# Dense layer 2: a third buffer of rounded and low parts, and rounding shared among three engines

## The reference

```python
edge_feat = gelu((x[src] + edge_attr) @ W_pre + b_pre) * bases
y = x + segment_sum(edge_feat, dst)
h = relu(bn(y @ W1 + b1))
h = relu(bn(h @ W2 + b2))          # bn: mean and variance over all nodes
x = layernorm(x + (y + h))
# second layer: messages over the edges by relation, a gate, an MLP, layernorm
```

## Time and profile before

| what | value |
| --- | --- |
| median of 3 runs | 2010.78 us (2007.58 to 2014.62) |
| the profiled execution's own time | 2016.65 us |
| its span, first to last instruction | 2014.9 us |
| mean granted TensorE clock | 0.962 of full speed |
| dense layer 2 in the span | about 626 to 934 us |
| GpSimd's last scatter | 678.64 us |

### The profile page before, as it was taken

How to read it: one execution, slowest core, us unless ns; L and a number is a source line. 1 busy time by engine, 2 the same in 40 slices (tenths; PEclk the granted TensorE clock), 3 DMA queues, 4 the chain that set the end, 5 groups by cost and what they waited for, 6 DMA issues and landing times. The chain is left out here.

```text
span 2014.9 us, 27432 instructions
## 1 busy us (share of the span) xinstructions
PE 1791.8 (89%) x8697; PEld 1398.7 (69%) x8697; DVE 1601.0 (79%) x2326; ACT 1295.1 (64%) x1818; POOL 1075.1 (53%) x1200
## 2 busy tenths in 40 slices
PE   4677589999998999999999999956999999999994
PEld 3465478888886776766666666635888888888883
DVE  4688456766767999997999999994888888888883
ACT  1434246566656898886888888862566666666663
POOL 7556446776785400001555555557776566654443
PEclk8899789999999999999999999987999999999997
DMA  9999999999995899994999999965654423222210
GB/s 343 368 352 393 363 357 339 337 342 330 342 236 135 244 350 343 333 344 157 351 388 384 389 412 392 385 247 137 174 157 138 118 89 92 92 83 79 65 41 29
DMA packets 190577, 516.22 MB, mean 256 GB/s; under 512 B 26757, under 2 KB 80111, under 8 KB 190178
## 3 DMA queue, kind: packets, MB, share of 16 engines
q1 hardware_dynamic: 132898, 389.66, 52.7%
q0 software_dynamic: 47136, 73.62, 16.2%
q10 hardware_dynamic: 10400, 51.20, 6.6%
HBM read 328.87 MB, written 241.07 MB: 283 GB/s over the span
## 5 line engine op out<-in xcount | busy, mean ns | idle before, releaser
L618 POOL DMA_INDIRECT scratch_y<-sums,k_target x196 | 313.4, 1599 | 156.1 <-issue 70.2
L1040 ACT ACTIVATE d_o<-d_u,d_free 128x256 f32<-128x256 f32 x392 | 203.1, 589 | 64.6 <-POOL d_free L1077 64.4
L1014 PEld LDWEIGHTS d_pN<-k_ident,d_r 128*128 128x128 f32 x1568 | 192.1, 193 | 52.1 <-issue 46.4
L1009 PE MATMUL d_pN<-d_y,d_free 128*128 128x512 f32 x392 | 192.0, 612 | 33.3 <-DVE d_u L1103 29.3
L821 ACT ACTIVATE d_part_h<-pT 128x1024 fp32r<-128x1024 f32 x98 | 100.5, 1026 | 150.7 <-PE pT L788 137.0
L1014 PE MATMUL d_pN<-k_ident,d_r 128*128 128x128 f32 x1568 | 192.7, 277 | 4.9 <-ACT d_r L1029 4.9
L882 DVE TENSOR_TENSOR d_part_l<-pT,d_part_h 128x1024 fp32r<-128x1024 f32 x98 | 119.9, 1225 | 85.8 <-ACT d_part_h L821 85.8
L1074 POOL TENSOR_TENSOR d_free<-d_free,k_minus_half 128x8 f32<-128x8 f32 (+1 forms) x100 | 163.6, 1636 | 0.2
L1103 DVE SCALAR_TENSOR_TENSOR d_u<-d_pN,d_free,k_base 128x256 f32<-128x256 f32 x392 | 161.0, 474 | 0.0
L256 POOL DMA_INDIRECT k_ring<-in_x,k_src x100 | 123.6, 1236 | 66.5 <-PE pT L284 37.8
L60 PE MATMUL pU<-d_part_h,k_w_h 128*128 128x512 f32 x296 | 125.9, 425 | 26.7 <-DVE d_part_l L882 13.7
(11 more groups left out here) (232 smaller groups left out, 5192.6 us busy)
## 6 DMA issues: line engine op xcount, KB each, us to landing
scratch_h<-d_h SPq DMA_DIRECT2D x168, 512.0 KB, 5.7
out<-d_o SPq DMA_DIRECT2D x97, 520.0 KB, 5.9
k_ring<-scratch_y SPq DMA_DIRECT2D x98, 512.0 KB, 7.8
d_y<-scratch_y SPq DMA_DIRECT2D x98, 512.0 KB, 7.7
scratch_y<-in_x ACTq DMA_DIRECT2D x25, 2000.0 KB, 20.2
d_h<-scratch_h SPq DMA_DIRECT2D x90, 512.0 KB, 7.0
k_ring<-scratch_h SPq DMA_DIRECT2D x78, 512.0 KB, 5.3
attr<-in_attr_t SPq DMA_DIRECT2D x25, 512.0 KB, 15.2
```

What stands on the lines that cost most here:

```text
L618: pool.indirect_dma_start(out=A["y"], out_offset=bass.IndirectOffsetOnAxis(ap=K.target[:, t:t + 1], axis=0), in_=K.sums[:, t], in_offset=N ...
L1009: pe.matmul(pN[k % 4][:, 2 * two:2 * two + 2].rearrange("p j f -> p (j f)"), twice[:], y[:, k % 4, two * 2 * F:(two + 1) * 2 * F], start=T ...
L1014: last = pe.matmul(pN[k % 4][:, j, cc * P:(cc + 1) * P], r[:, k % 4, cc, j * P:(j + 1) * P], K.ident[:], start=False, stop=j % 2 == 1 and ...
L1040: last = act.activation(o[:, k % 4, j, 0:F], u[:, k % 3, j], ACT.Identity, bias=nb[:, n, j:j + 1], scale=rs[:, n, J + j:J + j + 1])
```

## The change

From the first block of layer 2 on, there are three buffers of rounded and low parts instead of two, picked by (g - 98) % 3. The third pair, `third_h` and `third_l`, lies in the place of `sums`, behind the 64 tiles that hold blocks (tiles 64 to 71). Block 100, the first to use it, waits until the second scatter of these tiles has landed. A rounding waits for the product of three blocks before (`product` at g - 2) in place of that of two.

From the sixteenth block on (g >= 114), blocks with g % 3 == 1 are rounded by GpSimd instead of VectorE: 27 blocks, from 115 to 193. These copies stand in GpSimd's queue behind the last scatter and ahead of its last waits for them. VectorE's `parts` waits for GpSimd's semaphore there, as it does for ScalarE's, and does the low part of all blocks as before.

```diff
+POOL_FROM = 16
...
     part_h, part_l, h, held, r, _ = K.shared_second
+    third_h, third_l = K.shared_parts
...
-    hi2_scalar, hi2_vector = sem("hi2_scalar"), sem("hi2_vector")
+    hi2_scalar, hi2_vector, hi2_pool = sem("hi2_scalar"), sem("hi2_vector"), sem("hi2_pool")
...
+    def hi_on_pool(g):
+        return g % 3 == 1 and g >= NB + POOL_FROM
...
+    def parts_of(g):
+
+        at = (g - NB) % 3 if layer2(g) else g % 2
+        return (part_h[:, at], part_l[:, at]) if at < 2 else (third_h[:], third_l[:])
+
+    def wait_part(engine, g):
+
+        if g >= NB + 3:
+            engine.wait_ge(product, g - 2)
+        elif g == NB + 2:
+            for q in range(4):
+                engine.wait_ge(halved_in[q], 16 * (HELD_SUMS + 2))
+        else:
+            engine.wait_ge(product, g - 1)
...
         for t in range(early, ET):
             take_back(t)
+        for g in range(NB, 2 * NB):
+            if hi_on_pool(g):
+                pool.wait_ge(relu_done, g - NB + 1)
+                wait_part(pool, g)
+                pool.tensor_copy(parts_of(g)[0], r[:, g % 2]).then_inc(hi2_pool, 1)
...
         def hi2(g):
             if hi_on_scalar(g):
                 act.wait_ge(relu_done, g - NB + 1)
-                act.wait_ge(product, g - 1)
-                act.activation(part_h[:, g % 2], r[:, g % 2], ACT.Copy).then_inc(hi2_scalar, 1)
+                wait_part(act, g)
+                act.activation(parts_of(g)[0], r[:, g % 2], ACT.Copy).then_inc(hi2_scalar, 1)
...
         def parts(g):
             on_scalar = sum(hi_on_scalar(n) for n in range(NB, g + 1))
+            on_pool = sum(hi_on_pool(n) for n in range(NB, g + 1))
             if hi_on_scalar(g):
                 dve.wait_ge(hi2_scalar, on_scalar)
+            elif hi_on_pool(g):
+                dve.wait_ge(hi2_pool, on_pool)
             else:
                 dve.wait_ge(relu_done, g - NB + 1)
-                dve.wait_ge(product, g - 1)
-                dve.tensor_copy(part_h[:, g % 2], r[:, g % 2]).then_inc(hi2_vector, 1)
-                dve.wait_ge(hi2_vector, g + 1 - NB - on_scalar)
...
+                wait_part(dve, g)
+                dve.tensor_copy(parts_of(g)[0], r[:, g % 2]).then_inc(hi2_vector, 1)
+                dve.wait_ge(hi2_vector, g + 1 - NB - on_scalar - on_pool)
+            high, low = parts_of(g)
+            dve.tensor_tensor(out=low, in0=r[:, g % 2], in1=high.bitcast(F32), op=ALU.subtract).then_inc(lo_done, 1)
...
-            (K.sums,), K.shared_sums = same_place(
+            (K.sums,), (_, *K.shared_parts), K.shared_sums = same_place(
                 nc.sbuf_tensor, (("sums", [P, S.TC, F], F32),),
+                (("d_ahead", [P, HELD_SUMS * J * F], F32), ("d_third_h", [P, C, B], F32R), ("d_third_l", [P, C, B], F32R)),
```

More of the change, by code:

```diff
@@ L661, in dense12 @@
     early = ET * 3 // 4
-    assert HELD_SUMS * J <= early
+    assert (HELD_SUMS + 2) * J <= early
     passes = [(1, k) for k in range(NB)] + [(2, (NB - HOLD + n) % NB) for n in range(NB)]
@@ L803, in multiply @@
                     last = mm3(pe, bank(g)[:, oc], (K.w0_h[:, w, ic, cols], K.w0_l[:, w, ic, cols]),
-                               (part_h[:, g % 2, ic], part_l[:, g % 2, ic]), ic == 0, ic == C - 1)
+                               (high[:, ic], low[:, ic]), ic == 0, ic == C - 1)
             last.then_inc(product, 1)
@@ L886, in parts @@
             on_scalar = sum(hi_on_scalar(n) for n in range(NB, g + 1))
+            on_pool = sum(hi_on_pool(n) for n in range(NB, g + 1))
             if hi_on_scalar(g):
                 dve.wait_ge(hi2_scalar, on_scalar)
+            elif hi_on_pool(g):
+                dve.wait_ge(hi2_pool, on_pool)
             else:
                 dve.wait_ge(relu_done, g - NB + 1)
-                dve.wait_ge(product, g - 1)
-                dve.tensor_copy(part_h[:, g % 2], r[:, g % 2]).then_inc(hi2_vector, 1)
-                dve.wait_ge(hi2_vector, g + 1 - NB - on_scalar)
-            dve.tensor_tensor(out=part_l[:, g % 2], in0=r[:, g % 2], in1=part_h[:, g % 2].bitcast(F32),
-                              op=ALU.subtract).then_inc(lo_done, 1)
+                wait_part(dve, g)
+                dve.tensor_copy(parts_of(g)[0], r[:, g % 2]).then_inc(hi2_vector, 1)
+                dve.wait_ge(hi2_vector, g + 1 - NB - on_scalar - on_pool)
+            high, low = parts_of(g)
+            dve.tensor_tensor(out=low, in0=r[:, g % 2], in1=high.bitcast(F32), op=ALU.subtract).then_inc(lo_done, 1)
         def stats(g):
```

## The result

The changed kernel took 2022.07 us, the median of 14 runs (2018.9 to 2025.73); the kernel before, timed beside it, 2014.79 us (14 runs, 2007.58 to 2019.99). The ratio is 1.0037, with a 95% interval of 1.0027 to 1.0046: 7.3 us slower, against +13.0 in the forecast. The forecast's line between "within 0.3%" and "slower" lies inside that interval; by the medians it is 0.36%.

What follows compares the result with a forecast made beforehand. VectorE was taken to decide layer 2, tied with ScalarE's relu at every third block. Terms 14.9 - 2.0 + 2.6 - 2.5 = +13.0 us on 2010.78 gave 2023.8 us, range 2012 to 2046.

Steps and rivals of the forecast that it cites:

- the tie at the block of g % 3 == 1: Layer 2, block 136: VectorE's cast limited equally by its own work, free at 743.25 + 1.21, and ScalarE's relu, ending 744.40.
- The loop, x - 0.65 us for each GpSimd block: Layer 2's steady pattern: three blocks change from 9.08 us by GpSimd's copy time less 0.65; 27 x 0.55 = +14.9 us.
- 8.43 + x: Forecast time in us of three layer-2 blocks, summed along VectorE's statistics, ScalarE's queue, hand-overs and GpSimd's copy time x.
- What x is: Time of one 128x1024 copy on GpSimd, estimated from other instructions between 0.95 and 3.0 us, taken as 1.2.
- The two readings of the select's row: GpSimd's 128-column select, 282 ns: its 78 ns over the memset either fixed (copy 1.03 us) or per column (1.58).
- The third buffer, -2.0: Start of layer 2: VectorE casts block 100 without waiting for product 98, so block 101 starts about 2.0 us sooner.
- The first copy too early, +2.6 over the copy's own: Block 115: GpSimd's last scatter still runs when relu ends, so VectorE waits; +2.6 us over the copy's own 0.55.
- Paid back, -2.5: Blocks 151 and 183: VectorE's statistics merges partly lie in time ScalarE or GpSimd needs anyway; -2.5 us for both.
- No price: Buffer places, GpSimd's queue order with `twice`, semaphore waits, DMA and TensorE's clock were all to cost nothing.
- GpSimd at the memset's pace: Rival: GpSimd's copy takes 0.65 to 0.93 us, giving -1 to +6 us, 2010 to 2017; chance 0.19.
- The rival on the other side: Rival: GpSimd hands over sooner than VectorE's cast did, x under 0.65 us; at 0.4, -10 us, 2001; chance 0.07.
- The shared port: Rival: GpSimd's copies and VectorE's work meet at one port, each copy growing 0.92 us, +25, in all 2049; chance 0.07.

## Why the prediction came out as it did

**The total.** The 2022.07 us measured lie 1.7 us from the 2023.8 of the forecast, and that closeness is luck. The forecast stood on a median of 2010.78 us for the kernel before, and the 14 runs beside the changed one gave 2014.79, 4.0 more. The change itself was put at +13.0 and came to +7.3: the direction and the mechanism held, the size was 1.8 times too large.

**The bound.** Right: VectorE waits, and the tie at the block of g % 3 == 1 decides. The copy ends up in the loop whole, as the runs with half and twice the copy show.

**The loop, x - 0.65 us for each GpSimd block.** Right in form and nearly in size: 8.40 + x was measured where the text had 8.43 + x, as GpSimd takes over 0.06 us after the relu and not 0.08; the last 0.01 is in the rounding of the spacings.

**What x is.** This is the term that was mis-sized. I took 1.2 us; it is 1.043. Over 26 steps from hi2(117) to the end, the loop adds 0.36 us and not 0.55: 9.4 in place of 14.3 us. That is 4.9 of the 5.6 us between the forecast's sum and the 7.4 found here: 4.1 by x, and 0.8 by the 0.03 of the line above. The other terms below make up the rest. The two readings of the select's row that I stood between gave 1.03 and 1.58, and the lower was the right one. The half copy takes 616 ns and the whole 1043, 0.83 ns a column, which is the slope of the memset, with 0.19 us fixed. VectorE's cast of the same tile takes 678 ns, so the whole copy is 1.5 times as long on GpSimd. The Trainium skill's "GPSIMD Engine Reference" (section 4.1) calls one-input operations roughly line-rate, and this trace agrees, with 0.83 ns a column. The best loop that the Trainium skill gives there (section 3.1) would have meant an estimate of 1.54 us; this copy took 1.04, and the measurement decides.

**The third buffer, -2.0.** From the first low part to hi2(114) it is 48.65 us before and 47.34 after: -1.3.

**The first copy too early, +2.6 over the copy's own.** hi2(114) to hi2(117) is 11.59 us against 9.19: +2.4 with the copy's 0.36 in it. Right in place, 0.6 us too large over the copy's own. The forecast had put 0.3 us between the scatter and the copy; in the trace the copy ended 1.05 us after the scatter, with no such gap.

**Paid back, -2.5.** From hi2(117) to hi2(195) it is 246.94 us against 240.65: +6.3, where 26 steps of 0.36 would make 9.4. So 3.1 us came back. ScalarE's roundings show where. Those of blocks 153 and 156, over the merge at block 151, before and then after:

```profile
795.50 1.06 ACT L837 ACTIVATE d_part_h<-d_r 128x1024 fp32r<-128x1024 f32 x1
...
807.57 1.06 ACT L837 ACTIVATE d_part_h<-d_r 128x1024 fp32r<-128x1024 f32 x1 [1.09 <-PE pU L62]
```

```profile
797.26 1.06 ACT L863 ACTIVATE d_part_h<-d_r 128x1024 fp32r<-128x1024 f32 x1
...
807.55 1.06 ACT L863 ACTIVATE d_part_h<-d_r 128x1024 fp32r<-128x1024 f32 x1
```

That step takes 12.07 us before and 10.29 after, and the one over the second merge 10.68 and 9.94: 2.5 us less, or 3.2 counted from a step that is 0.36 longer. All the other steps are 9.44 or 9.45 us, but for the last (9.54).

The sum of the measured parts: -1.3 + 2.4 + 6.3 = +7.4 us.

**No price.** Neither `twice`, nor the wait on `halved_in`, nor the clock cost anything that shows: the granted clock was 1.00 in every stretch of 690 to 930 us, what follows the layer is within its spread, and the run with three buffers alone was not slower.

**The rivals.** GpSimd at the memset's pace was nearly what came, though 1.04 us with the fixed part lies above the limit of 0.93 that I had set for it. The rival on the other side came true only where half of the work was left out, at x = 0.62, near the 0.65 from which it was to decide. The shared port had next to no part in the changed kernel: its copies take 1043 ns by the median, as VectorE stands waiting while they run. Two were longer: the first, beside GpSimd's own scatter, and one behind the second merge, where VectorE was late and the copy began beside a low part, which reads two tiles in SBUF (904.66 to 905.88):

```profile
905.41 1.38 POOL L801 CAST d_third_h<-d_r 128x1024 fp32r<-128x1024 f32 x1 [8.40 <-ACT d_r L855]
```

In the run with relu ahead of out in the changed kernel five copies met a low part so, one of them here:

```profile
892.54 1.35 POOL L801 CAST d_third_h<-d_r 128x1024 fp32r<-128x1024 f32 x1 [8.64 <-ACT d_r L855]
```

```profile
891.78 1.21 DVE L924 TENSOR_TENSOR d_part_l<-d_r,d_part_h 128x1024 fp32r<-128x1024 f32 x1
```

The copy took 1.35 us and ended 0.90 after the low part did. The five began 0.26 to 0.50 us ahead of the low part's end, and took 1.16 to 1.39, but each of them ended 0.89 to 0.91 us after it: only some 0.14 us of a copy got done beside a low part, however long they lay together. The Trainium skill's "SBUF — State Buffer" has it so: one side holds the port for its whole instruction. The price here is 0.1 to 0.35 us, paid after the stop at block 115 and after each merge; of the other copies only the first was longer, beside a scatter.

## What to carry to other kernels

Before you move work off the busiest engine, look at what its next instruction waits for. If that is the very producer which the moved work also needs, then the move only replaces one duration by another in the same loop, and a slower engine makes it worse. Here the load was not the fault but the order in another engine's queue: two lines exchanged on ScalarE were worth 15 us, and only then did the third buffer (6 us of the layer, where it had been worth 2.6) and GpSimd (5 us, with its later start) pay. An engine that has another task first should get its first block when that task is through.

## What the runs showed of the hardware

A GpSimd copy of 128x1024 float32 to float32r takes 1043 ns and one of 128x512 takes 616: 0.83 ns a column and 0.19 us fixed. Beside its own last scatter the first copy shows 1.60 us, and it ended 1.05 after that scatter. GpSimd took a block over 0.06 us after ScalarE's relu and VectorE followed 0.04 us after the copy, so the hand-over is not what costs. A copy that began beside a low part of VectorE ended 0.9 us after it, whether it had begun 0.26 or 0.50 us ahead of that end. From 700 to 790 us DMA moved 381 GB/s with the exchanged order in the changed kernel, though its engines had shown 0.97 of their time busy at 347 GB/s in the same stretch before.
